# One graph layer on one core: the score buffer behind x's parts, the last rounding one tile later, and every second tile normalised on ScalarE

## The reference, cut to what matters

```python
xn = layernorm(x)                                  # x: 2500 x 1024, eps 1e-5
x = x + gnn(xn) + mix(xn)
x = x + ffn(layernorm(x))

gnn: support = xn @ W; out = segment_sum(support[src] * edge_weight, dst)     # 42500 edges
mix: q, k, v = xn @ Wq.T + bq, xn @ Wk.T + bk, xn @ Wv.T + bv                 # 16 heads of 64
     q, k = q / norm(q), k / norm(k)               # norms over the whole arrays
     phi(t) = exp(weights . t) * exp(-sum(t * t) / 2) / 8
     s = sum_m(phi(q) * phi(k)) per row and head; out = s * v / s
ffn: bitlinear(silu(bitlinear(r, w_gate)) * bitlinear(r, w_up), w_down)       # inner 512
bitlinear(x, w): rows of x rounded to 127 levels of their largest value, w to -1, 0, 1
```

## Time and profile before

| | |
|---|---|
| time, median of 3 runs | 1653.69 us (1653.36 to 1654.15) |
| the profiled execution | 1655.15 us, of which the span is 1653.4 us |
| TensorE busy | 1623.9 us, 98% of the span, 7680 matmuls |
| VectorE busy | 1132.4 us, 68% |
| ScalarE busy | 497.1 us, 30% |
| GpSimd busy | 713.9 us, 43% |
| mean granted clock of TensorE | 0.995 |

### The profile page before, as it was taken

One profiled execution on the slowest core, in us unless ns is written; L12 is line 12 of the kernel. 1 busy time (PEld: TensorE's weight loads), 2 busy tenths in 40 slices (PEclk: granted clock), 3 DMA queues, 4 the chain that ended last, 5 costly groups with the idle time before them and its releaser, 6 DMA issues.

```text
span 1653.4 us, 21995 instructions
## 1 busy us (share of the span) xinstructions
PE 1623.9 (98%) x7680; PEld 1336.2 (81%) x7680; DVE 1132.4 (68%) x2622; ACT 497.1 (30%) x640; POOL 713.9 (43%) x577
## 2 busy tenths in 40 slices
PE   7999999899999999999999999999999999999998
PEld 6899999688878888887888888888888888887665
DVE  7887793476787776656555566677757667576796
ACT  4644311222121111114211113333423324233554
POOL 2011555677777777777678605533130120300200
PEclk9999999899999999999999999999999999999999
DMA  9999888765686756557866656577383563742954
GB/s 315 352 410 354 294 269 261 204 139 126 134 210 149 198 131 151 148 142 168 230 148 130 137 154 196 162 189 197 101 195 116 124 161 99 158 127 76 240 157 125
DMA packets 164010, 304.94 MB, mean 184 GB/s; under 512 B 62856, under 2 KB 103624, under 8 KB 163945
## 3 DMA queue, kind: packets, MB, share of 16 engines
q1 hardware_dynamic: 77853, 204.77, 38.9%
q0 software_dynamic: 80272, 82.55, 24.3%
q10 hardware_dynamic: 5820, 16.88, 2.9%
HBM read 202.88 MB, written 101.24 MB: 184 GB/s over the span
## 4 chain that ended last, share of the span: by engine, by line
PE 76%; DMA 12%; DVE 5%; issue 4%; POOL 2%; SPq 1%; ACT 0%; DVEq 0%; POOLq 0%; ACTq 0%
PE PS L402 24%; PE PS L404 24%; PE PS L403 24%; DMA A_dense<-zeros 5%; DMA A_dense<-wtot,cell 5%; POOL A_dense L747 2%; PE PS L1886 2%; PE PS L1916 1%; DVE fin L1572 1%; DMA X<-in_x 1%; DVE stats L1157 1%; DMA rt<-z 1%; DVE hid L1546 0%; DVE ring L1176 0%; DVE h_sc L1549 0%
## 5 line engine op out<-in xcount | busy, mean ns | idle before, releaser
L747 POOL DMA_INDIRECT A_dense<-wtot,cell x333 | 537.6, 1615 | 217.4 <-DMA A_dense<-wtot,cell 123.0
L402 PE MATMUL PS<-AL,SH 125*128 125x500 f32 x784 | 306.3, 391 | 0.0
L404 PE MATMUL PS<-AH,SH 125*128 125x500 f32 x784 | 305.1, 389 | 0.0
L403 PE MATMUL PS<-AH,SL 125*128 125x500 f32 x784 | 304.6, 389 | 0.0
L402 PE MATMUL PS<-WL,xtH 128*125 128x512 f32 x640 | 252.5, 394 | 0.7 <-DVE xtL L1296 0.7
L403 PE MATMUL PS<-WH,xtL 128*125 128x512 f32 x640 | 252.1, 394 | 0.0
L404 PE MATMUL PS<-WH,xtH 128*125 128x512 f32 x640 | 251.9, 394 | 0.0
L1033 ACT ACTIVATE SH<-S 125x1024 fp32r<-125x1024 f32 x98 | 104.0, 1061 | 333.0 <-PE PS L404 333.0
L1410 DVE TENSOR_TENSOR SL<-S,SH 125x1024 fp32r<-125x1024 f32 x98 | 119.6, 1220 | 120.3 <-ACT SH L1033 120.1
L404 PEld LDWEIGHTS PS<-AH,SH 125*128 125x128 f32 x784 | 147.8, 189 | 31.4
L403 PEld LDWEIGHTS PS<-AH,SL 125*128 125x128 f32 x784 | 147.1, 188 | 31.0
(11 more groups left out here) (202 smaller groups left out, 2660.2 us busy)
## 6 DMA issues: line engine op xcount, KB each, us to landing
A_dense<-zeros POOLq DMA_DIRECT2D x40, 1280.0 KB, 9.1
xt<-xnT SPq DMA_DIRECT2D x60, 500.0 KB, 6.2
Araw<-A_dense SPq DMA_DIRECT2D x100, 250.0 KB, 2.7
Aside<-A_dense SPq DMA_DIRECT2D x100, 250.0 KB, 3.0
keyrow<-key_rows SPq DMA_DIRECT2D x42, 512.0 KB, 4.2
ewrow<-weight_rows SPq DMA_DIRECT2D x42, 512.0 KB, 5.5
xnT<-XT ACTq DMA_DIRECT2D x20, 500.0 KB, 8.2
zx<-in_x SPq DMA_DIRECT2D x20, 448.0 KB
```

Of the source, the lines that this page charges most:

```text
L402: nc.tensor.matmul(o, lh, rl, start=start, stop=False)
L403: nc.tensor.matmul(o, ll, rh, start=False, stop=False)
L404: return nc.tensor.matmul(o, lh, rh, start=False, stop=stop)
L747: pool.indirect_dma_start(cells[m], bass.IndirectOffsetOnAxis(cell[:, col:col + 1], 0), wtot[:, col:col + 1], None, compute_op=ALU.add).th ...
```

## The change

It has three parts.

- **Layout.** x's parts now begin at `late`; `ex` and `zx` stand behind them, up to the end of the region, where `zeros` lies. `bdk` moves to the tail of `Gs`, the three first source buffers begin at `late`. VectorE's wait for the strips of zeros moves from t = 0 ahead of tile 1's low part to t = 1, between the wait for tile 1's products and the second write of `ex`.
- **Second tile of a pair.** From the pair (2, 3) on, VectorE normalises the first tile only. It makes `shift` = -mean * rstd for the second, and ScalarE applies it, Identity(x * rstd + shift), after it has evicted the transposed rows of the tile two before (`normalise_second(n + 2)` for odd n). Both engines wait for the count of normalised tiles, so that it stays in order. `s_rstd` is counted twice a pair, and the waits on it follow.
- **Last rounding.** `ROUNDED_AT` is (8, 10, 12, 14): the fourth largest value moves from turn 12 to turn 13, the fourth rounding from 13 to 14, with `scales_back` behind it, after `add_down(13)`. ScalarE's `integers` for that tile moves to turn 14 as well.

```diff
--- before.py
+++ after.py
@@ -78,7 +78,7 @@
 RIGHT_SCALES = [[(0, 128, 2.0), (128, 256, 1.0), (256, 512, 2.0)], [(0, 390, 2.0)]] + [[(0, 128, 1.0), (128, 390, 2.0)]] * 5
 NORM_BANK = (5, 1)
 X_BANK = (0, 4)
-ROUNDED_AT = (8, 10, 12, 13)
+ROUNDED_AT = (8, 10, 12, 14)
 STATS_AT = (4, 6)
 NL, NR = len(LEFT_WIDTHS), len(RIGHT_WIDTHS)
 NB = NL + NR
@@ -151,6 +151,7 @@
     mv = small("mv", [P, TILES, 2])
     std = small("std", [P, TILES])
     rstd = small("rstd", [P, TILES])
+    shift = small("shift", [P, TILES])
     stats = small("stats", [P, GT, 2, 6])
     group_mv = small("group_mv", [P, GT, 2])
     norms = small("norms", [P, 8, 2])
@@ -211,16 +212,16 @@
     brows = e1k("brows", [P, 2, P])
     iedge = e1k("iedge", [P, 2, ROWS_C], I32)
     wst = e1k("wst", [P, D])
-    bdqk = (bdq, zone("E1f", at, END_AT)("bdk", [P, KT, P]))
     late = E_AT + 20 * D
     assert at <= late
-    ex = zone("E1x", late, END_AT)("ex", [P, 2, D])
-
-    zx = zone("E2x", late, END_AT)("zx", [P, 2, D])
-    e2 = zone("E2", cursor["E2x"], END_AT)
+
+    e2 = zone("E2", late, END_AT)
     xt = e2("xt", [P, 2, KT, ROWS])
     xtH, xtL = zip(*[[e2(f"xt{x}{i}", [P, KT, ROWS], F32R) for x in "HL"] for i in range(2)])
-    e2s = zone("E2s", cursor["E2x"], cursor["E2x"] + 4 * 4 * KT * ROWS)
+    bdqk = (bdq, zone("E1f", at + 4 * (NB * 512 - KT * P), END_AT)("bdk", [P, KT, P]))
+    zx = zone("E2x", cursor["E2"], END_AT)("zx", [P, 2, D])
+    ex = zone("E1x", cursor["E2"], END_AT)("ex", [P, 2, D])
+    e2s = zone("E2s", late, late + 4 * 4 * KT * ROWS)
     SH0, SL0, SH1 = [e2s(f"{n}_first", [P, D], F32R) for n in ("SH0", "SL0", "SH1")]
     e2b = zone("E2b", E_AT, END_AT)
     fwb = e2b("fwb", [P, 2, D])
@@ -849,6 +850,12 @@
             act.wait_ge(s_st, b)
             nc.scalar.activation(std[0:ROWS, cols], mv[0:ROWS, cols, 1], ACT.Sqrt, bias=eps[0:ROWS, :]).then_inc(s_std, 1)
 
+        def normalise_second(t):
+            act.wait_ge(s_rstd, t + 1)
+            act.wait_ge(s_xn, t)
+            nc.scalar.activation(X[0:ROWS, t, :], X[0:ROWS, t, :], ACT.Identity, scale=rstd[0:ROWS, t:t + 1],
+                                 bias=shift[0:ROWS, t:t + 1]).then_inc(s_xn, 1)
+
         def high_of_rows(n):
             act.wait_ge(s_xn, min(n, TILES - 1) + 1)
             if n >= 3:
@@ -885,6 +892,8 @@
             if n % 2 == 0 and n + 2 < TILES:
                 deviations(n + 2, n + 4)
             transposed_rows(n)
+            if n % 2 and n + 2 < TILES:
+                normalise_second(n + 2)
             if n:
                 write_transposed(n - 1)
             if n == 3:
@@ -1161,13 +1170,17 @@
 
         def normalise(a, b):
             cols = slice(a, b)
-            n = b if b <= 2 else b // 2 + 1
-            dve.wait_ge(s_std, n)
+            dve.wait_ge(s_std, b if b <= 2 else b // 2 + 1)
+            n = b if b <= 2 else b - 1
             nc.vector.reciprocal(rstd[0:ROWS, cols], std[0:ROWS, cols]).then_inc(s_rstd, 1)
             dve.wait_ge(s_rstd, n)
-            for t in range(a, b):
-                nc.vector.tensor_scalar(X[0:ROWS, t, :], X[0:ROWS, t, :], mv[0:ROWS, t, 0:1], rstd[0:ROWS, t:t + 1],
-                                        ALU.subtract, ALU.mult).then_inc(s_xn, 1)
+            if b > 2:
+                t = a + 1
+                nc.vector.scalar_tensor_tensor(shift[0:ROWS, t:b], mv[0:ROWS, t, 0:1], -1.0, rstd[0:ROWS, t:b],
+                                               ALU.mult, ALU.mult).then_inc(s_rstd, 1)
+                dve.wait_ge(s_xn, a)
+            nc.vector.tensor_scalar(X[0:ROWS, a, :], X[0:ROWS, a, :], mv[0:ROWS, a, 0:1], rstd[0:ROWS, a:a + 1],
+                                    ALU.subtract, ALU.mult).then_inc(s_xn, 1)
 
         def low_of_rows(n):
             dve.wait_ge(s_hi, n + 1)
@@ -1310,14 +1323,14 @@
         dve.wait_ge(s_bb, 2)
         for t in range(TILES):
             i = t % 2
-            if t == 0:
-                for c in range(2):
-                    dve.wait_ge(s_Azero[c], 16 * A_PITCH // P)
             low_of_tile(1 - i, t // 2 + i)
             if t < KT:
                 dve.wait_ge(s_w2h, t + 1)
                 nc.vector.tensor_tensor(WL[:, t, :], stage[:, t % 2, :], WH[:, t, :].bitcast(F32), ALU.subtract).then_inc(s_w2l, 1)
             dve.wait_ge(s_mm[i], t // 2 + 1)
+            if t == 1:
+                for c in range(2):
+                    dve.wait_ge(s_Azero[c], 16 * A_PITCH // P)
             if t >= 2:
                 dve.wait_ge(s_red[i], t // 2)
             nc.vector.tensor_tensor(ex[0:ROWS, i, :], two_banks(i)[0:ROWS], bb[0:ROWS, :], ALU.add).then_inc(s_ta[i], 1)
@@ -1440,7 +1453,7 @@
         def inverse_deviation(g):
             dve.wait_ge(s_std, g + NP + 2)
             nc.vector.reciprocal(rstd[0:ROWS, 0:GT], std[0:ROWS, 0:GT]).then_inc(s_rstd, 1)
-            dve.wait_ge(s_rstd, g + NP + 2)
+            dve.wait_ge(s_rstd, g + TILES + 1)
 
         def largest_r(g, d):
 
@@ -1597,12 +1610,14 @@
                 round_r(GROUPS - 1, ROUNDED_AT.index(t))
             if t + 1 in ROUNDED_AT:
                 largest_r(GROUPS - 1, ROUNDED_AT.index(t + 1))
-        dve.wait_ge(s_f6, TILES * 4 - 1)
-        scales_back(slice(TILES - GT, TILES))
-        dve.wait_ge(s_fb, 2)
         for t in range(TILES - GT - 2, TILES - 2):
             hidden(t // 2, t % 2)
             add_down(t - 1)
+            if t == ROUNDED_AT[-1]:
+                round_r(GROUPS - 1, GT - 1)
+                dve.wait_ge(s_f6, TILES * 4 - 1)
+                scales_back(slice(TILES - GT, TILES))
+                dve.wait_ge(s_fb, 2)
         hidden(HALF - 1, 0)
         hidden(HALF - 1, 1, 2)
         for t, bank in ((TILES - 3, 4), (TILES - 2, 0), (TILES - 1, 2)):
```

## The result

| | before | after |
|---|---|---|
| time, median (range) | 1653.77 us (1653.36 to 1654.15, 4 runs) | 1642.73 us (1641.07 to 1643.33, 4 runs) |
| ratio | | 0.9932, 95% interval 0.9915 to 0.9949 |
| the profiled execution | 1655.15 us, span 1653.4 | 1642.87 us, span 1641.1 |

The forecast was 1641.5 us, in a range of 1640.4 to 1645.2. The change makes the kernel 11.0 us faster by the medians, 8.4 to 14.1 us by the interval (the ratios are taken over all runs and are not those of the medians). The sum said 12.2, which lies inside that interval. Direction and mechanism held. The times alone don't show that a term was too large; the traces of the experiments point at one, the first.

What follows compares the result with a forecast made beforehand. TensorE, busy 98% of the span, was taken as the bound. Terms 10.35 + 0 + 1.87 = 12.2 us took the profiled 1655.15 to 1642.9, or 1641.5 against the median; range 1640.4 to 1645.2.

Steps and rivals of the forecast that it cites:

- Part 1: -10.35 forecast: Map stage: without the zeros wait ahead of tile 1's low part, its eviction comes 10.35 us earlier; range -10.4 to -7.3.
- 7.5 is idleness and 2.85 the half clock: Map tile 1: split of the 10.35 us gain into TensorE's standing still and its return at 1.2 GHz.
- It holds nothing: Map stage: the moved wait is reached at 321.4, the strip landed by 316.3, so it costs no time.
- Part 2: 0 forecast: First stage: ScalarE normalising second tiles leaves TensorE the bound, 0.3 us spare a pair; range -0.7 to +2.0.
- rival 4: First stage: Identity displaces Sqrt, so ScalarE's table changes twice a pair; 15.9 us slower, 1657.4; chance 0.02.
- Rival 2: First stage: ScalarE's hand-over becomes the bound; 0.3 us over on 7 pairs costs 2, 1643.5; twice that, 1645.6; chance 0.13.
- Part 3: -1.87 forecast: Last stage: rounding moved to tile 14 brings tile 15's hidden transposes from 1623.33 to 1621.46; range -2.0 to 0.
- rival 1: Last stage: a turn of 5.98 us is 0.3 longer, hidden 14 and 15 wait again; at worst 1643.4; chance 0.09.
- Rival 3: Map stage: tile 2's x load takes 16 us, its parts ready 2 us after TensorE asks; 1643.5; chance 0.06.
- Rival 5: Map stage: tile 1 still waits for the zeros and only the end pays; 1651.8; chance 0.03.
- the gain taken back by the scatter: After the map stage: a wait on GpSimd's scatter takes the gain back, within 0.2%; margin forecast 11.3 us; chance 0.03.

Runs made afterwards that it cites:

- part 2 alone: Kernel before plus only ScalarE's normalising of each pair's second tile, with its shift and waits: 1654.07 us against 1654.63, ratio 1.0007.
- parts 1 and 3 without it: Changed kernel with VectorE again normalising both tiles of a pair: 1642.86 us, ratio 0.9935.
- part 3 alone: Kernel before with only the fourth last rounding moved to turn 14: 1651.90 us against 1654.63, ratio 0.9984.
- moving the strips: Kernel before with the second matrix's zero strips issued two at a time ahead of the first ten scatter turns: 1649.54 us, ratio 0.9972.
- the one with the wait kept: Kernel before with the new buffer layout but the wait for zero strips left at t = 0: 1654.34 us against 1653.91, ratio 1.0003.
- the burst held back: Kernel before with SyncE waiting for all zero strips ahead of key rows, edge weight rows and x's tile 2: 1648.39 us against 1653.91, ratio 0.9962.
- the fillers: Kernel before with 28 more matmuls of 512 columns on TensorE between map tiles 0 and 1: 1651.88 us against 1653.91, ratio 0.9990.
- x's loads first: Changed kernel with SyncE's two bias row loads moved behind the load of x's pair 5: 1642.25 us, ratio 0.9937.
- part 1 alone: Kernel before with only the new layout and the zero-strip wait moved from t = 0 to t = 1: 1644.67 us against 1654.63, ratio 0.9957.

## Why the prediction was right, and where it was off

**Part 1: -10.35 forecast.** Right in each step for the execution that I read: the low part of tile 1 at once, tile 1's eviction 10.35 earlier, tile 2 in time (forecast 315.8 on the clock of before; 314.37 + 1.15 = 315.5), the waits for the scatter met. The step that is too large is "7.5 is idleness and 2.85 the half clock": I took one execution's wait as the kernel's. With the same wait in the code "tile 1" is 32.58, 31.34, 31.37 and, once, 22.22. Two of those three stalls are worth 31.35 - 22.23 = 9.1, and that is near what part 1 gave by the medians (10.0). With 9.1 the sum would be 9.1 + 1.8 = 10.9, so this term can account for the 1.2 us between 12.2 and 11.0; the intervals are too wide to show it. In the trace of before two things were longer than in the two others: TensorE stood for 7.33 us, not 6.71 and 6.89, and the low level lasted longer (0.50 over all of 313.5 to 323.5), so that tile 1 took 14.2 us and not 13.4 to 13.6. The warning was in sight: the profiled execution stood 1.46 above the median, and I subtracted that offset from both ends instead of asking in which wait it lay. "It holds nothing" came true with less room than I gave it: I took the strip's landing of 316.3 over from before, and it came at 317.7.

**Part 2: 0 forecast, none seen**, by part 2 alone and by parts 1 and 3 without it, to about 1 us. The working held in detail. The group of the new instruction in the changed kernel (busy us, mean ns, idle before), and the table loads of the line that answers the earlier trace rows:

```profile
L856 ACT ACTIVATE X<-X,shift,rstd 125x1024 f32<-125x1024 f32 x9 | 11.1, 1233 | 0.0
...
L1055 ACT ACT_TABLE_LOAD x2 | 2.6, 1283 | 0.0
```

1233 ns where I took 1.2 us, nine of them, and no table load at `L851` or `L856`: rival 4 doesn't exist. (The Trainium skill, "ScalarE: Activation LUTs", What ACT_TABLE_LOAD costs, gives 186 ns and 0.833 a column with 93 more for each pointer operand; an estimate by that page is 1225 ns, and the trace agrees.) The low part of tile 10 follows the eviction of transposed tile 7 by 9.1 us (50.30 - 41.19), as I had it before and after (51.05 - 41.84 = 9.2). The shift took 0.08 to the next start, not 0.2. Rival 2 had the right chain, but not the right price: of a hand-over 0.74 longer it would have made 0.44 on each of seven pairs, 3.1 us, and it cost 1.7, at three pairs; one 0.30 longer cost 0.4, at the keys' pair.

**Part 3: -1.87 forecast, -1.8 in the trace of part 3 alone** (91.16 - 89.35), -1.5 to -1.8 with the other parts. TensorE's transposes of hidden rows at the end, which answer:

```profile
1593.37 0.39 PE L1914 MATMUL PS<-ident,hq 125*128 125x125 bf16 x4
...
1599.22 0.38 PE L1914 MATMUL PS<-ident,hq 125*128 125x125 bf16 x4
...
1605.07 0.39 PE L1914 MATMUL PS<-ident,hq 125*128 125x125 bf16 x4
...
1611.15 0.39 PE L1914 MATMUL PS<-ident,hq 125*128 125x125 bf16 x4
```

5.85, 5.85 and 6.08 apart: the 1.45 and 0.26 us of lateness are gone, and 0.23 of the foreseen kind is back at tile 15 (I had 0.13). VectorE's turns, worked out as 5.98 and 6.28, came at 1595.15, 1601.13 and 1607.40: 5.98 and 6.27. So rival 1, a turn 0.3 longer, didn't come.

**The other rivals.** Rival 3: tile 2's load gave its low part at 314.37, in time. Rival 5: no trace without the wait at t = 0 has TensorE waiting there. The case that I had put last, the gain taken back by the scatter, needs a scatter over 5 us later than in the tightest trace; moving the strips shows what it then does.

**Open.** Why GpSimd's last strip leaves at 299 in one execution and at 305 in another isn't settled; each turn waits for landings of its own transfers, and T0 moves as well, by 3.7 us over the eleven traces. In the first stage, nine of the eleven have a stretch at a granted clock of 0.50 somewhere between 10 and 37 us (the one with the wait kept has two). The other two, the burst held back and the second one of the changed kernel, are at 1.00 from 8 to 76 and have the earliest T0, 297.12 and 297.69. So these stretches are likely a part of the spread of T0; the rest of it is open.

## What to carry to other kernels

A wait on a transfer that ends a chain of other transfers has no single price: read how far its release stands from the moment that matters, ask what is issued beside the last transfer, and take a second trace before you price it: the profiled execution here stood 1.4 us above its median, and its wait was the longest seen. The cheapest cure is to move the wait to where its buffer is first overwritten; it took away the cost, and 27 runs of four kernels without it lie within 3.3 us, while reordering the transfers paid elsewhere. When work moves to another engine at a net of 0, measure the spare of the hand-over by lengthening it, and read it turn by turn: here it was none at one pair, 0.35 us at two and over 0.7 at four.

## What the runs showed of the hardware

- TensorE's clock: 3.56, 4.74, 6.71, 6.89 and 7.33 us of standing still were all followed by the 1.2 GHz level, with the first matmul shown at 0.78 or 0.79; 0.44 us, with the fillers ahead of it, was not. Of the shorter waits in the first stage 2.43 us was followed by it (x's loads first, 33 to 36 us), and 2.31 us was not (part 2 alone, 1.00 from 30 to 38). At tile 1 of the map stage the tile then took 13.4 to 14.2 us from its first matmul to its eviction against 11.4, so the half clock cost 2.0 to 2.7 us.
- The last strip of 1.28 MB lands 6.1 us after its issue in the two traces in which it leaves 4.4 us ahead of SyncE's next loads; with these loads held back its waiter goes on after 6.3. Where three loads of together 1.5 MB from SyncE are asked for at about the same time, it lands after 10.0 and 10.6 with the old wait, and after 13.5 and 13.7 in part 1 alone and the changed kernel.
- SyncE's seventeenth DMA issue, 8 to 9 us into the kernel, takes 4.7 to 6.9 us of SyncE's own time, in thirteen traces with a load of bias rows in that place and in one with a load of x (4.97); most issues before it take 0.3 to 0.7.
